# Filling the second adjacency table in four batches of edges instead of eight, and starting its scatters at batch five

## The chip, the cores and the metric

The kernel runs on one core of one Trainium2 chip. The metric is the device time of one execution in microseconds (us). Three executions of the kernel before took 3864.45, 3867.06 and 3872.6 us; the median is 3867.06 us.

## The reference, cut to what matters

3125 nodes with 256 features pass through four residual blocks: a graph convolution network of two layers, a mixture of experts that routes each node to two of eight, a gated graph network of five layers (a GRU), and a small two-expert feed-forward block. Both graph blocks sum messages over the same 50000 edges:

```
ew  = clip(abs(edge_weight), 1e-06)                   # first graph block
agg = segment_sum((dis[row] * ew * dis[col])[:, None] * xw[row], col)
agg = segment_sum(m[src] * edge_weight[:, None], dst) # third block, five times
```

## The kernel before, in words

The kernel turns both sums into dense products. It builds two tables in device memory, each 3200 by 3200 float32: `plane_a` (the weights made absolute, plus the identity, for the first block) and `plane_w` (the signed weights, for the third). A table is first filled by plain transfers, `plane_a` with zeros and a diagonal, `plane_w` with zeros, and then edge weights are added to single elements by indirect transfers that accumulate. The 50000 edges lie as 128 partitions by 392 columns (`ET`). One indirect transfer (a scatter) takes one column, 128 edges. 14 columns (`G`) are a batch, so there are 28 batches (`NB`). Within a batch, edges with the same pair of nodes are summed beforehand, so that no element is added to twice in it, and a batch on a table starts only when the batch before it on that table has landed.

Who does what up to 945 us, with the names in the code:

- VectorE compares the keys of a batch with each other (L1353 to L1361), TensorE sums the weights of equal keys, ScalarE evicts the sums, and VectorE writes the slots and values (`place`, L1364 to L1372) and raises `placed`. ScalarE also starts one transfer per batch that broadcasts the keys of a later batch to all partitions (`load_keys`, L922, 896 KB each).
- SyncE's queue holds, in order: the edges, the fill of `plane_a` (25 transfers, L332), the input x, and then the fill of `plane_w`: 100 transfers of 400 KB (L336 to L339, 128 rows of 3200 bytes each). Fill number n waits until n // FB + 1 batches of `plane_a` have landed (`scat_a`), with FB = 13: thirteen fills per batch of edges, eight batches of edges, the last with nine fills. Behind them SyncE waits until all 28 batches are placed (L347), and then loads and stores the halves of the experts' weights (`load_part`, `w_split`, L345 to L361), whose stores are also held back by counts of landed batches. Then it waits for all of `plane_a`'s scatters (L371) and streams the table into the ring `gring_lo` (L379), from which the first graph block is computed.
- GpSimd issues the scatters. Its loop over the batches (L510 to L518) waits for `placed`; from batch `FIRST_W` = 9 on it issues one single scatter to `plane_w` (L506); then it waits for the landing of the previous batch on `plane_a` and issues fourteen scatters to `plane_a` (L500). At batch 9 exactly it first waits until all 100 fills of `plane_w` have landed (`filled_w`, L513). So 19 scatters to `plane_w` are issued inside the loop. After the loop 233 more follow (up to 252 = G * W1, L519), and the last 140 are issued between the steps of the experts' block (L542).

Batches are numbered from 0 here, as in the code.

Of the kernel before, what the change touches and what calls it, by code (L numbers as in the profile page):

```python
# [25 lines left out]
NB = ET // G  # L26
UP = G * (G + 1) // 2
W1 = 18
FB, FIRST_W = 13, 9
BP, P0 = 18, 4  # L30
WB = 3
FULL = 112
# [1927 lines left out]
```

## Time and profile before

| | us |
|---|---|
| median of three runs | 3867.06 |
| the profiled execution's own time | 3872.27 |
| its span in the profile | 3870.7 |
| TensorE busy (matmul) | 3051.9 (79%) |
| VectorE busy | 2375.8 (61%) |
| ScalarE busy | 1530.7 (40%) |
| GpSimd busy | 1414.4 (37%) |

The span is the time from the first to the last instruction of the profiled execution; its own time is 1.6 us longer. Busy shares are averages over stages: during the first 945 us the tables are built, from 945 to some 1460 us the first graph block runs, to some 1940 us the experts, to 3650 us the GRU, and then the last block. A share over the whole span therefore says little of what limits a stage.

### The profile page before, as it was taken

The numbers are of one execution on the slowest core, as the hardware profiler recorded it, in microseconds if no ns is written. First come the engines' busy times: TensorE is split into PE (matmuls) and PEld (weight loads), VectorE is DVE, ScalarE is ACT, GpSimd is POOL, SyncE is SP. The second block draws the span as 40 slices with busy tenths as digits, with TensorE's granted clock in tenths as the row PEclk, the third lists the DMA queues.
The fourth block names the chain that finished last, engine by engine and source line by source line (L and its number), as shares of the span: only waits on it lengthen the run. The fifth ranks groups of instructions, "written<-read, shape, count | busy, mean of one in ns | idle before, by whom it ended". The sixth has DMA issues, their size and how long they took to land.

```text
span 3870.7 us, 54544 instructions
## 1 busy us (share of the span) xinstructions
PE 3051.9 (79%) x18100; PEld 2747.6 (71%) x18101; DVE 2375.8 (61%) x5044; ACT 1530.7 (40%) x3100; POOL 1414.4 (37%) x921
## 2 busy tenths in 40 slices
PE   2455454201999994999949999999999999999798
PEld 2444453101888883888849988998998899899677
DVE  7999996511787876555575555455545555555447
ACT  2344342110444552333334444444444444444255
POOL 1577888788877774878800000000000000000000
PEclk9999998655999996999979999999999999999889
DMA  9877335684667655535263333343433343344000
GB/s 395 265 226 196 38 48 118 188 255 79 177 166 204 181 129 172 136 86 136 33 225 125 129 119 128 119 131 117 134 127 119 127 129 122 126 132 131 37 31 29
DMA packets 378074, 538.46 MB, mean 139 GB/s; under 512 B 125779, under 2 KB 283642, under 8 KB 374458
## 3 DMA queue, kind: packets, MB, share of 16 engines
q1 hardware_dynamic: 251076, 487.82, 37.1%
q0 software_dynamic: 119088, 19.33, 8.8%
q10 hardware_dynamic: 7750, 29.17, 2.1%
q8 instruction: 100, 1.64, 0.2%
q14 instruction: 60, 0.49, 0.0%
HBM read 398.99 MB, written 137.25 MB: 139 GB/s over the span
## 4 chain that ended last, share of the span: by engine, by line
PE 44%; DVE 4%; DMA 1%; ACT 1%; issue 0%; SPq 0%; POOL 0%; ACTq 0%; DVEq 0%
PE bank L607 43%; DVE ring_lo L1702 1%; PE bank L786 1%; PE bank L855 1%; DMA yg_end<-chosen 0%; DVE gates_sb L1728 0%; ACT ring_hi L1107 0%; DVE gates_sb L1727 0%; DVE res_b L1814 0%; DVE xT L1729 0%; DVE v_lo L1759 0%; DVE stats L1780 0%; DVE stats L1817 0%; DVE nat L1789 0%; DMA past_res<-chosen 0%
## 5 line engine op out<-in xcount | busy, mean ns | idle before, releaser
L506 POOL DMA_INDIRECT plane_w<-pair,slot x392 | 658.0, 1679 | 188.4 <-issue 128.4
L500 POOL DMA_INDIRECT plane_a<-pair,slot x392 | 624.1, 1592 | 267.6 <-issue 123.4
L607 PE MATMUL bank<-ring_hi,h_hi 128*128 128x448 f32 x1750 | 652.7, 373 | 60.9 <-DVE ring_lo L1702 55.5
L1702 DVE TENSOR_TENSOR ring_lo<-ring_lo,ring_hi 128x448 fp32r<-128x448 f32 x875 | 522.8, 621 | 220.4 <-ACT ring_hi L1107 219.9
L1107 ACT ACTIVATE ring_hi<-ring_lo 128x448 fp32r<-128x448 f32 x875 | 497.3, 576 | 384.6 <-PE bank L607 378.0
L607 PE MATMUL bank<-ring_lo,h_hi 128*128 128x448 f32 x1750 | 643.5, 368 | 0.0
L607 PE MATMUL bank<-ring_hi,h_lo 128*128 128x448 f32 x1750 | 643.1, 367 | 0.0
L554 POOL DMA_DIRECT2D v_lo<-gru_v x5 | 3.6, 722 | 1388.1 <-PE bank L607 1311.9
L607 PE MATMUL bank<-gring_hi,hs_hi 128*128 128x512 f32 (+2 forms) x700 | 261.6, 374 | 256.6 <-DVE gring_lo L1417 256.6
L607 PEld LDWEIGHTS bank<-ring_hi,h_hi 128*128 128x128 f32 x1750 | 331.1, 189 | 89.8 <-DVE h_lo L1769 49.3
L1720 DVE SCALAR_TENSOR_TENSOR gates_sb<-bank,bhh,gates_sb 128x448 f32<-128x448 f32 x70 | 47.9, 685 | 516.7 <-ACT gates_sb L1131 516.7
L607 PEld LDWEIGHTS bank<-ring_hi,h_lo 128*128 128x128 f32 x1750 | 331.1, 189 | 27.6
L607 PEld LDWEIGHTS bank<-ring_lo,h_hi 128*128 128x128 f32 x1750 | 331.6, 189 | 25.9
L983 ACT ACTIVATE gring_hi<-gring_lo 128x512 fp32r<-128x512 f32 (+2 forms) x350 | 199.8, 584 | 340.4 <-DMA gring_lo<-plane_a 169.9
L607 PEld LDWEIGHTS bank<-gring_hi,hs_hi 128*128 128x128 f32 x700 | 132.5, 189 | 278.2 <-issue 256.8
L1417 DVE TENSOR_TENSOR gring_lo<-gring_lo,gring_hi 128x512 fp32r<-128x512 f32 (+2 forms) x350 | 207.6, 630 | 182.9 <-ACT gring_hi L983 174.0
L579 PE MATMUL bank<-parts,eq 128*128 x392 | 58.6, 169 | 324.5 <-DVE hit_hi L1361 302.1
L579 PEld LDWEIGHTS bank<-parts,eq 128*128 128x128 bf16 x392 | 39.3, 105 | 328.8 <-issue 328.8
L930 ACT ACTIVATE off_lo<-row,dlo_neg 128x128 f32<-128x128 f32 x392 | 151.7, 387 | 297.9 <-DVE hit_hi L1361 257.5
L607 PE MATMUL bank<-gring_lo,hs_hi 128*128 128x512 f32 (+2 forms) x700 | 257.4, 368 | 0.0
L607 PE MATMUL bank<-gring_hi,hs_lo 128*128 128x512 f32 (+2 forms) x700 | 257.3, 368 | 0.0
L1130 ACT ACTIVATE gates_sb<-bank,brz 128x448 f32<-128x448 f32 x70 | 44.4, 634 | 474.0 <-PE bank L607 474.0
(349 smaller groups left out, 6742.2 us busy)
## 6 DMA issues: line engine op xcount, KB each, us to landing
ring_lo<-plane_w SPq DMA_DIRECT2D x175, 1120.0 KB, 5.5
gring_lo<-plane_a SPq DMA_DIRECT2D x50, 1280.0 KB
plane_a<-nat SPq DMA_DIRECT2D x25, 1600.0 KB, 43.4
plane_w<-nat SPq DMA_DIRECT2D x100, 400.0 KB
w_hl<-w_split SPq DMA_DIRECT2D x16, 2048.0 KB
part_in<-in_L_ffn_W SPq DMA_DIRECT2D x16, 1024.0 KB
w_split<-part_hi SPq DMA_DIRECT2D x16, 1024.0 KB
w_split<-part_lo SPq DMA_DIRECT2D x16, 1024.0 KB
```

The lines of the kernel that those rows point to most:

```text
L500: g_.indirect_dma_start(out=plane, out_offset=bass.IndirectOffsetOnAxis(slot[:, t:t + 1], 0), in_=pair[:, k, t:t + 1], in_offset=None, com ...
L506: g_.indirect_dma_start(out=plane_w, out_offset=bass.IndirectOffsetOnAxis(slot[:, n:n + 1], 0), in_=pair[:, 0, n:n + 1], in_offset=None, c ...
L579: mm(ps_sum[c][:, g, :], eq_row(c, g, g, g + 1), parts(g, 8), start=True, stop=(g == G - 1))
L607: last = mm(ps, lhs[x], rhs[y], start=start and n == 0, stop=stop and n == 2)
L786: last = tr(turned_tile(i, t)[:, k * 128:(k + 1) * 128], xT[:, k, t * 128:(t + 1) * 128], ident[:, :])
L930: A(off_lo[:, g % 2, :], row[:, :], ACT.Square, bias=dlo_neg[:, bass.ds(n * G + g, 1)]).then_inc(lo_apart, 1)
L983: A(gring_hi[:, n % RH, 0:w_], gring_lo[:, n % RS, 0:w_].bitcast(FP32), ACT.Copy).then_inc(ring_h, 1)
L1107: A(ring_hi[:, t % HS, :], ring_lo[:, t, :].bitcast(FP32), ACT.Copy).then_inc(hi_rdy, 1)
L1130: A(gr[:, j, :], gate_ps[0][:, 0:GW], ACT.Sigmoid, bias=brz[:, j:j + 1])
L1417: V.tensor_tensor(gring_lo[:, n % RS, 0:w_], gring_lo[:, n % RS, 0:w_].bitcast(FP32), gring_hi[:, n % RH, 0:w_].bitcast(FP32), ALU.subtrac ...
L1702: V.tensor_tensor(ring_lo[:, t, :], ring_lo[:, t, :].bitcast(FP32), ring_hi[:, t % HS, :].bitcast(FP32), ALU.subtract).then_inc(lo_rdy, 1)
L1720: link(V.scalar_tensor_tensor(gr[:, j, :], gate_ps[3][:, 0:GW], bhh[:, 2 * KD + j:2 * KD + j + 1], gr[:, j, :], ALU.add, ALU.mult))
```

## The change

Two constants on one line:

```
-FB, FIRST_W = 13, 9
+FB, FIRST_W = 25, 5
```

With FB = 25, fill n of `plane_w` waits for n // 25 + 1 landed batches: 25 fills each after batches 0, 1, 2 and 3 have landed. With FIRST_W = 5 GpSimd waits for `filled_w` ahead of batch 5 and issues one scatter to `plane_w` ahead of each of the batches 5 to 27, 23 in all; 229 follow behind the loop. The number of fills, of scatters and of bytes is unchanged, and so is everything from the 253rd scatter to `plane_w` on.

## Rows read from the trace of the kernel before

**Rows 1.** Waits from 870 to 960 us: who waited for whom, total, times, longest.

```profile
PE bank L607 <- DVE gring_lo L1417: 251.2, 1, 251.2
ACT gring_hi L983 <- DMA gring_lo<-plane_a: 98.9, 2, 98.2
SPq L379 <- DMA plane_a<-pair,slot: 65.1, 1, 65.1
```

**Rows 2.** Timeline, last `plane_a` scatter and the first ring load (start, duration, engine).

```profile
941.33 1.55 POOL L500 DMA_INDIRECT plane_a<-pair,slot  x1 [0.30 <-issue]
...
944.34 24.53 SPq L379 DMA_DIRECT2D gring_lo<-plane_a  x5
```

**Rows 3.** Timeline of GpSimd: batch starts and pauses; in brackets the idle time before.

```profile
154.30 1.55 POOL L500 DMA_INDIRECT plane_a<-pair,slot  x1 [4.19 <-DMA plane_a<-pair,slot]
...
182.04 1.55 POOL L500 DMA_INDIRECT plane_a<-pair,slot  x1 [2.11 <-DMA plane_a<-pair,slot]
...
238.19 1.55 POOL L500 DMA_INDIRECT plane_a<-pair,slot  x1 [2.65 <-DMA plane_a<-pair,slot]
...
249.25 1.56 POOL L500 DMA_INDIRECT plane_a<-pair,slot  x1 [3.96 <-issue]
...
269.67 1.55 POOL L500 DMA_INDIRECT plane_a<-pair,slot  x1 [2.17 <-DMA plane_a<-pair,slot]
...
353.37 1.56 POOL L500 DMA_INDIRECT plane_a<-pair,slot  x1 [2.29 <-DMA plane_a<-pair,slot]
358.09 1.55 POOL L500 DMA_INDIRECT plane_a<-pair,slot  x1 [3.15 <-issue]
...
372.70 1.56 POOL L500 DMA_INDIRECT plane_a<-pair,slot  x1 [1.96 <-issue]
...
383.84 1.55 POOL L506 DMA_INDIRECT plane_w<-pair,slot  x1 [0.30 <-issue]
385.70 1.55 POOL L500 DMA_INDIRECT plane_a<-pair,slot  x1 [0.30 <-issue]
...
413.48 1.55 POOL L500 DMA_INDIRECT plane_a<-pair,slot  x1 [0.30 <-issue]
```

**Rows 4.** DMA issues of the page: target, source, count, KB each.

```profile
plane_w<-nat SPq DMA_DIRECT2D x100, 400.0 KB
...
front<-key_rows ACTq DMA_DIRECT2D x14, 896.0 KB
```

**Rows 5.** Windows over fill bursts: length, busy per engine, clock, DMA share, GB/s.

```profile
153.60:170.20 16.60, 5.87 (x29) 5.75 (x28) 16.45 (x44) 4.87 (x17) 13.46 (x9) 1.00 1.00 321
181.30:201.80 20.50, 10.54 (x133) 9.95 (x133) 19.68 (x60) 8.54 (x29) 16.71 (x11) 1.00 1.00 305
...
237.50:253.70 16.20, 5.65 (x27) 5.53 (x26) 16.20 (x43) 4.78 (x16) 10.03 (x7) 1.00 0.98 329
...
sum 144.50, PE 68.73 PEld 65.15 DVE 141.10 ACT 57.72 POOL 111.94; mean PE 8.59 PEld 8.14 DVE 17.64 ACT 7.21 POOL 13.99
```

**Rows 6.** The same view inside two bursts, without their beginnings.

```profile
155.20:170.20 15.00, 4.26 (x21) 4.15 (x21) 14.85 (x39) 3.37 (x12) 12.56 (x9) 1.00 1.05 336
...
300.00:315.00 15.00, 6.57 (x43) 6.37 (x40) 15.00 (x35) 5.36 (x18) 12.56 (x9) 1.00 1.08 356
```

**Rows 7.** Timeline of ScalarE's queue, key loads (six from first to last).

```profile
170.01 0.34 ACTq L922 DMA_DIRECT2D xT<-key_rows  x1
...
274.67 0.34 ACTq L922 DMA_DIRECT2D front<-key_rows  x1
```

**Rows 8.** The page's slices of 96.8 us, GB/s moved.

```profile
GB/s 395 265 226 196 38 48 118 188 255 79 177 166 204 181 129 172 136 86 136 33 225 125 129 119 128 119 131 117 134 127 119 127 129 122 126 132 131 37 31 29
```

**Rows 9.** Timeline of GpSimd, two `plane_w` scatters around the stage of the experts' weights.

```profile
633.98 1.55 POOL L506 DMA_INDIRECT plane_w<-pair,slot  x1 [0.31 <-issue]
...
859.83 1.55 POOL L506 DMA_INDIRECT plane_w<-pair,slot  x1 [0.30 <-issue]
```

**Rows 10.** Timeline of GpSimd, the last scatter behind the loop and the first gather.

```profile
1480.16 1.55 POOL L506 DMA_INDIRECT plane_w<-pair,slot  x1 [0.30 <-issue]
1505.31 1.03 POOL L525 DMA_INDIRECT xT<-tokens,idx_x  x1 [23.61 <-DVEq L1631]
```

**Rows 11.** Waits from 0 to 1000 us, VectorE for key loads.

```profile
DVE eq L1359 <- DMA front<-key_rows: 15.8, 1, 15.8
```

## The prediction

> **What bounds the kernel now.** I read the waits around the start of the first graph block first, since all of the edited code lies ahead of it. TensorE stands still for 251.2 us until its first ring tile is ready, ScalarE has waited 98.2 us for the first ring load, and SyncE's queue has stood 65.1 us on one thing only, the landing of `plane_a`'s scatters [rows 1]. The reader is to see that nothing else is late there: whatever moves the last `plane_a` scatter (941.33) moves the first ring load, three microseconds behind it [rows 2], and with it all that follows, one for one, while the move is under some 65 us. So the whole question is when GpSimd issues its 392 scatters to `plane_a`.
>
> Then the timeline of GpSimd, batch by batch. A scatter occupies it for 1.55 us and the next follows 0.3 us later, so fourteen take 25.9 us, and the next batch waits some 2 us more for the landing: batch 1 begins at 154.30 and batch 2 at 182.04, 27.74 us later. Batches 5, 6 and 7 together take from 269.67 to 353.37, 27.9 us each. From batch 9 on a `plane_w` scatter stands in front, yet from 385.70 to 413.48 it is 27.78 us: fifteen issues of 1.85 us, and the landing wait has gone. Thus one `plane_w` scatter per batch is free, because it fills a wait [rows 3]. In batches 4 and 8 there are three pauses (3.96, 3.15 and 1.96 us) that no releaser explains; all lie in or just behind a burst of fills.
>
> Last the windows over the fills. The eight bursts take 144.5 us together from their gates to their last data; a burst of thirteen takes 16.2 or 16.6 us where no key load falls into it, 20.5 us where one does [rows 5]. Today a burst ends before its batch of edges does, and the DMA engines are idle of it until the next gate; and GpSimd reaches its wait for the fills (ahead of 383.84) with all 100 long landed, so that it pauses 0.3 us [rows 3].
>
> **The change part by part.**
>
> 1. *The fills become one stream.* The first gate stays at 153.6. The next ones open when batches 1, 2 and 3 have landed, every 28 us, but 25 fills need more: thirteen took 14.6 to 15.0 us of flow (bursts of rows 5 less a lead-in of 1.6, from 153.6 to where the flow of [rows 6] begins), that is 1.14 us a fill or 28.5 us for 25, and with one key load about 33. So each gate opens before the DMA engines are through with the previous 25, and there is no gap. Length of the stream, in two ways. By times: 1.6 + 100 x 1.14 + six key loads [rows 7] x 4.1 (20.5 - 16.4) = 140.2 us. From the measured total: 144.5, less seven lead-ins of 1.6, plus one key load more than the five that fall into today's bursts, = 137.4 us. I take 139; it ends at 292.6. Bounds: with 1.12 us a fill and 3 us a key load, 132 us; with nothing saved by chaining and the sixth key load, 148.6 us. As a check by bytes: 100 x 400 KB and 6 x 896 KB [rows 4] are 46.5 MB, which is 334 GB/s, between the 305 and 329 of whole bursts and the 336 and 356 inside them [rows 5, 6].
>
> 2. *GpSimd's wait for the fills comes while they run.* Batch 4 is issued from about 240 to 270 (today 238.19 to 267.5, with its pause). There GpSimd now stands until the stream has landed, 292.6 and 1 us for the semaphore (bounds 0 and 2.7, the longest ordinary landing wait of [rows 3]). Behind it in its queue are all later scatters to both tables. One `plane_w` scatter (1.85 us) goes first, and batch 5 begins at 295.4 instead of 269.67: **+25.8 us**. What the long stream does to batches 1 to 4 costs nothing extra: even if their landing waits grow, they have until 292.6, that is 34.6 us a batch against 28. For the same reason the pause of 3.96 us in batch 4 does not count.
>
> 3. *Four more `plane_w` scatters in the loop*, ahead of batches 5 to 8. They fill the landing wait: three periods of 27.78 instead of 27.90, **-0.3 us**. Without that cover each would cost 1.85 us.
>
> 4. *No fills beside batches 5 to 8.* Batch 8 now lasts 32.33 us (353.37 to 385.70) and would last 27.78: **-4.5 us** if the two pauses come from the fills, 0 if not. I take -4.5, since between batches 9 and 17, without fills, none is seen.
>
> 5. *Four fewer scatters behind the loop*, 7.4 us of GpSimd: worth nothing. The last of them is issued at 1480.16 and GpSimd then idles 23.61 us until VectorE has the indices [rows 10]. Bounds 0 and -7.4.
>
> 6. *The others.* VectorE is ahead of the scatters and was held by a key load once only, at the start, 15.8 us [rows 11]; with two key buffers a load that takes a few us longer in the stream is hidden behind a batch of comparisons of 21 us (0; a bound of +3). SyncE has nothing behind the fills until all batches are placed, far later. The stage of the experts' weights slows the scatters: from 633.98 to 859.83 there are seven periods of 32.3 us, 31 us over the ordinary [rows 9]. Its transfers now meet the chain up to a batch earlier, but are the same in number and mostly held by counts of landed batches: 0, bounds -8 and +4.
>
> Sum: 25.8 - 0.3 - 4.5 = **+21 us**. On the profiled execution's 3872.27 us this gives 3893; it lies 5.2 us above the median of 3867.06, for which the same sum gives **3888 us**.
>
> The Trainium skill, page "DMA: Bandwidth & Descriptors", section "Specifications", puts the limit of one core's traffic with device memory at about 358 GB/s; the trace agrees so far, with 356 GB/s as the most inside a burst [rows 6]. By that figure the stream, 46.5 MB, would last an estimated 130 us, and the change would cost about 12 us.
>
> **The rivals.**
>
> - *The stream is hidden.* Not slower than before. Small bursts may understate what a long run of fills reaches: the fill of `plane_a`, longer rows in a run of 25 transfers, moved 395 GB/s over the whole first slice [rows 8]. At that rate 46.5 MB need 118 us and the stream ends at 273; batch 5 starts at about 276, +6, and less 4.8 the result is +1: 3868 us. It decides the matter if a fill takes under about 1.0 us in the stream. Against it: 3200-byte rows never passed 356 GB/s here, in any of eight bursts. The same page, section "Bandwidth", gives 425 GB/s for a 16 MB transfer and says that batching brings transfers nearer the peak; by that figure the stream would be an estimated 109 us and wholly covered. No run here shows that rate.
> - *The delay is partly made good in the weights' stage.* If the loads that VectorE's progress starts (at 643 us, unmoved) collide with fewer batches, up to 8 of the 31 us vanish: +13, 3880 us. Against it: the last stores wait for counted batches and move along.
> - *Scatters and fills hinder each other.* While the weights move, a batch takes 32.3 us on average, though they are far fewer bytes than the fills. If the stream stretches to 148.6 us and the pauses of batch 8 stay, it is 302.2 + 1 + 1.85 - 269.67 - 0.3 = +35: 3902 us. For it: bursts with a key load move only 305 GB/s. Against: the bursts were measured with the scatters in them.
> - *GpSimd's time counts after all.* With the hidden stream and 7.4 us fewer behind the loop on the path: +1 - 7.4 = -6, and -8 with better luck in the weights' stage: 3859 us. The 23.61 us of idleness speak against it.
>
> **How the numbers follow.** Forecast (+12 to +29) 0.70; scatters hindered (+30 and more) 0.09; delay partly made good (+8 to +12) 0.05; hidden stream 0.12; GpSimd's time 0.04. A measurement of this kernel can tell 0.2%, 7.7 us, from no change. So slower 0.84, same 0.12, faster 0.04. Its own range is 3879 to 3896; for eight in ten over all cases I take 3869 to 3902, from the hidden stream's edge to the hindered one.
>
> **What would show it.** Right: the fills of `plane_w` run from 153.6 to about 293 at 330 to 340 GB/s without a gap; GpSimd idles some 20 us ahead of its first `plane_w` scatter, put down to the fills; batches 5 to 8 follow at 27.8 us without pauses; the last `plane_a` scatter is issued at about 962 and the first ring load at 965; all later stages keep their lengths. Wrong: no idle time ahead of that scatter (hidden stream), batches 1 to 4 that last beyond 34.6 us, pauses that stay in batch 8, or weights' periods other than 32 us on average.

## The result and the profile after

The changed kernel takes 3885.92 us (median of six runs, 3880.66 to 3892.61) against 3866.84 us of the kernel before in runs beside it: +19.1 us, a ratio of 1.0043 with a 95% interval of 1.0032 to 1.0053. It is slower by 0.4%, clear of the noise, and the forecast of 3888 us and its range of 3869 to 3902 us hold. The profiled execution spans 3891.0 us against 3870.7, +20.3.

The waits from 870 to 990 us of the changed kernel (who waited for whom, total, times, longest) show the same picture as [rows 1]: the first block stands and waits for the ring, and for nothing else.

```profile
PE bank L607 <- DVE gring_lo L1417: 248.5, 1, 248.5
...
ACT gring_hi L983 <- DMA gring_lo<-plane_a: 100.3, 3, 98.2
```

The last `plane_a` scatter comes at 958.84 and the first ring load at 961.82, 17.5 us later than in [rows 2]. Now GpSimd's timeline of the changed kernel, the lines that answer to [rows 3] (start, duration, in brackets the idle time before and what ended it):

```profile
153.19 1.55 POOL L500 DMA_INDIRECT plane_a<-pair,slot  x1 [3.47 <-DMA plane_a<-pair,slot]
...
185.57 1.55 POOL L500 DMA_INDIRECT plane_a<-pair,slot  x1 [6.76 <-DMA plane_a<-pair,slot]
...
220.95 1.55 POOL L500 DMA_INDIRECT plane_a<-pair,slot  x1 [9.75 <-DMA plane_a<-pair,slot]
...
253.64 1.55 POOL L500 DMA_INDIRECT plane_a<-pair,slot  x1 [7.06 <-DMA plane_a<-pair,slot]
...
267.41 1.56 POOL L500 DMA_INDIRECT plane_a<-pair,slot  x1 [6.67 <-issue]
...
290.19 1.55 POOL L506 DMA_INDIRECT plane_w<-pair,slot  x1 [4.54 <-DMA plane_w<-nat]
292.04 1.55 POOL L500 DMA_INDIRECT plane_a<-pair,slot  x1 [0.30 <-issue]
...
376.64 1.55 POOL L500 DMA_INDIRECT plane_a<-pair,slot  x1 [0.30 <-issue]
...
404.58 1.55 POOL L500 DMA_INDIRECT plane_a<-pair,slot  x1 [0.44 <-DMA plane_a<-pair,slot]
```

The reader is to see two things. Batch 5 begins at 292.04, 22.4 us later than before, close to the forecast 295.4. But GpSimd stood only 4.54 us for the fills, where the prediction expected some 20. The time had gone already: the landing waits ahead of batches 2, 3 and 4 are 6.76, 9.75 and 7.06 us where they were 2.11, 2.25 and 2.65 (+16.6 us), and the pause in batch 4 is 6.67 us, not 3.96 (+2.7). Then batch 8 lasts 27.94 us (376.64 to 404.58) instead of 32.33: its two pauses are gone.

The windows over the stream of fills (length, busy per engine, clock, DMA share, GB/s) of the changed kernel show a nearly steady flow; SyncE issues the 100 fills from 152.5 to 279.4, and the data end at about 288:

```profile
155.00:185.00 30.00, 14.15 (x150) 13.44 (x150) 29.59 (x78) 11.63 (x39) 20.11 (x13) 1.00 1.09 343
185.00:215.00 30.00, 14.21 (x219) 13.25 (x220) 28.75 (x94) 11.88 (x40) 21.66 (x14) 1.00 1.08 354
215.00:245.00 30.00, 17.41 (x186) 16.56 (x183) 29.18 (x79) 14.51 (x49) 20.12 (x13) 1.00 1.02 335
...
285.00:290.00 5.00, 0.00 (x0) 0.00 (x0) 5.00 (x10) 0.09 (x1) 0.65 (x1) 1.00 0.68 187
290.00:295.00 5.00, 0.00 (x0) 0.00 (x0) 4.97 (x19) 0.00 (x0) 4.20 (x3) 1.00 0.16 0
```

Windows of 30 us hide something that shorter ones show. The flow falls where one group of 25 fills ends and the next begins: slightly at 185, and to a quarter at 220 and at 253:

```profile
219.50:221.00 1.50, 1.50 (x9) 1.50 (x8) 1.50 (x4) 1.17 (x4) 0.05 (x1) 1.00 0.25 99
...
252.50:254.00 1.50, 0.84 (x7) 0.66 (x7) 1.08 (x8) 0.39 (x1) 0.36 (x1) 1.00 0.26 102
```

SyncE issued the 25th fill at 178.0 and the 26th only at 184.86; the third and fourth groups begin at 220.23 and 252.92. So each group waited at its gate until the batch of edges beside the group before had landed, and that batch landed just when that group's data were through (185.57, 220.95 and 253.64 above are the moments at which GpSimd goes on). In this stretch a batch of edges lasts as long as its 25 fills.

Behind the ring load everything keeps its length to within 2 us (last load of the `plane_w` ring 3590.6, before 3574.3: +16.3) until the end of the GRU. There, in these two executions, two groups of 36 products take 10.33 and 8.94 us, where the kernel before took 7.58 and 7.69; the chains of waits of the changed kernel show

```profile
3638.23 10.33 PE bank L607 x36
...
3651.32 8.94 PE bank L607 x36
```

and the window over them (its last three numbers are the granted clock, the DMA share and GB/s)

```profile
3638.00:3661.00 23.00, 20.00 (x80) 17.74 (x80) 1.48 (x3) 1.82 (x4) 0.00 (x0) 0.79 0.28 120
```

The granted clock is 0.79 on average there, so that part of the window ran at the lower of the two levels (1.2 and 2.4 GHz), and 1.00 over the same groups of the kernel before. That is 4.0 us of the span's 20.3, seen in one execution each. Whether it belongs to the change is not shown: of the runs below, the profiles of e1 (10.40 and 9.15 us) and e3 (9.14 and 8.97) show it in both groups, those of e5 and e6 in the first, those of e2, e4, e7 and e8 in neither, and what sets it no run tells.

### The profile page after: what moved, and what is told of

Read it like the earlier page. It is cut to its first block, busy times and chain, and to the rows that moved or that the text cites. A ratio compares the mean times of both kernels' runs of the same rounds, so it can differ in the third digit from the quotient of the medians.

```text
span 3891.0 us, 54540 instructions
## 1 busy us (share of the span) xinstructions
PE 3059.7 (79%) x18100; PEld 2753.8 (71%) x18101; DVE 2375.3 (61%) x5044; ACT 1530.5 (39%) x3100; POOL 1420.1 (36%) x921
## 4 chain that ended last, share of the span: by engine, by line
PE 44%; DVE 4%; DMA 1%; ACT 1%; issue 0%; SPq 0%; POOL 0%; ACTq 0%; DVEq 0%
PE bank L607 43%; DVE ring_lo L1702 1%; PE bank L786 1%; PE bank L855 1%; DMA yg_end<-chosen 0%; DVE gates_sb L1728 0%; ACT ring_hi L1107 0%; DVE gates_sb L1727 0%; DVE res_b L1814 0%; DVE xT L1729 0%; DVE v_lo L1759 0%; DVE stats L1780 0%; DVE stats L1817 0%; DVE nat L1789 0%; DMA fb<-in_L_ffn_b1T 0%
```

## The experiments

Eight kernels, each timed against the kernel before on the same chip. Each changes only the lines shown and computes everything.

| kernel | edit (FB, FIRST_W) | last `plane_a` scatter | median us | before | ratio (95%) |
|---|---|---|---|---|---|
| before | 13, 9 | 941.33 | | | |
| changed | 25, 5 | 958.84 | 3885.92 | 3866.84 | 1.0043 (1.0032 to 1.0053) |
| e1 | 25, 9 | 959.11 | 3888.58 | 3868.70 | 1.0046 (1.0033 to 1.0059) |
| e2 | 13, 8 | 954.65 | 3883.67 | 3868.70 | 1.0040 (1.0027 to 1.0053) |
| e3 | 7, 5, FW = 1 | 976.56 | 3903.27 | 3868.70 | 1.0082 (1.0069 to 1.0095) |
| e4 | 13, 17, gates 8 later | 945.49 | 3880.83 | 3868.70 | 1.0026 (1.0015 to 1.0036) |
| e5 | 20, 6 | 944.68 | 3872.36 | 3869.92 | 1.0008 (0.9999 to 1.0016) |
| e6 | 17, 7 | 936.54 | 3869.52 | 3869.92 | 0.9999 (0.9991 to 1.0008) |
| e7 | 15, 8 | 937.37 | 3867.42 | 3869.92 | 0.9995 (0.9987 to 1.0004) |
| e8 | 13, 8, gates 1 earlier | 937.99 | 3867.09 | 3869.92 | 0.9994 (0.9985 to 1.0002) |

The third column is from each profile, one execution each; it leaves out the variation that later stages add. The expectations give times against a kernel before of 3867 us. Beside the runs it took 3868.70 (e1 to e4) and 3869.92 (e5 to e8), so differences are compared, not times.

### e1: the stream without the early wait

```
-FB, FIRST_W = 13, 9
+FB, FIRST_W = 25, 9
```

> FB = 25, FIRST_W = 9: the fills as in the changed kernel, but GpSimd's wait for them stays ahead of batch 9. Theory W (the prediction's): the price is GpSimd's wait for the fills, and batches 1 to 4 are slowed only because there is slack; then batch 5 begins within 5 us of the kernel before (270 to 275) and the time is 3864 to 3870 us. Theory L, formed on the changed kernel's trace, where batches 1 to 4 took 32.4, 35.4, 32.7 and some 36 us and GpSimd waited only 4.5 us for the fills: the price is the landing waits (6.8, 9.8 and 7.1 us instead of 2.1 to 2.7) and the pause of 6.7 us beside the stream; then batch 5 begins at 287 to 291 and the time is 3880 to 3885 us.

Measured: +19.9 us, the cost of the whole change; theory L had said +13 to +18. GpSimd's timeline:

```profile
186.00 1.55 POOL L500 DMA_INDIRECT plane_a<-pair,slot  x1 [6.70 <-DMA plane_a<-pair,slot]
...
221.53 1.57 POOL L500 DMA_INDIRECT plane_a<-pair,slot  x1 [9.90 <-DMA plane_a<-pair,slot]
...
253.94 1.55 POOL L500 DMA_INDIRECT plane_a<-pair,slot  x1 [6.71 <-DMA plane_a<-pair,slot]
...
267.76 1.56 POOL L500 DMA_INDIRECT plane_a<-pair,slot  x1 [6.72 <-issue]
...
289.61 1.55 POOL L500 DMA_INDIRECT plane_a<-pair,slot  x1 [3.59 <-DMA plane_a<-pair,slot]
...
376.47 1.55 POOL L500 DMA_INDIRECT plane_a<-pair,slot  x1 [1.87 <-issue]
...
391.10 1.56 POOL L500 DMA_INDIRECT plane_a<-pair,slot  x1 [1.96 <-issue]
```

There is no wait for the fills here, yet batches 1 to 3 last as long as in the changed kernel, batch 4 takes 35.67 us where the kernel before took 31.48, and batch 5 begins only 2.4 us earlier than in the changed kernel. Theory W falls: taking the wait away gives back 2.4 us at batch 5, of which nothing is left at batch 9, since here the two pauses of batch 8 are back (1.87 and 1.96 us) although no fill runs then. Theory L holds: the long stream makes the scatters land late, and that alone costs what the change costs. The gates show the same lock-step as in the changed kernel: the second to fourth groups of fills start at 185.28, 220.81 and 253.22.

### e2: the wait alone

```
-FB, FIRST_W = 13, 9
+FB, FIRST_W = 13, 8
```

> FB = 13, FIRST_W = 8: the fills in eight bursts as before, GpSimd's wait for them one batch earlier, while the last nine fills run. Theory W: GpSimd idles from 351 until these have landed at about 369, some 16 us, less the 4.5 us of pauses in batch 8 that now fall into the wait: +11 to +14 us, 3878 to 3881 us. Theory L says the same of this wait, since here it is no longer than the fills; if a wait of GpSimd there did not reach the end of the kernel, the time would be 3862 to 3870 us.

Measured: +15.0 us, a little more than the 11 to 14 expected. GpSimd's first `plane_w` scatter:

```profile
368.75 1.55 POOL L506 DMA_INDIRECT plane_w<-pair,slot  x1 [16.34 <-DMA plane_w<-nat]
```

The bursts and the landing waits are nearly as before (2.1 to 3.5 us), and the wait of 16.34 us moves the last `plane_a` scatter by 13.3 us. So a wait of GpSimd there does reach the end in full; in the changed kernel it is merely short, because the late landings have used up the same time. The wait and the late landings are two ways to the same delay, and each is enough alone.

### e3: longer rows, a faster stream

```
-FB, FIRST_W = 13, 9
+FB, FIRST_W = 7, 5
-FW = 4
+FW = 1
```

> FW = 1, FB = 7, FIRST_W = 5: plane_w is filled by 25 transfers of 1600 KB with rows of 12800 bytes, seven per batch of edges in four batches. Theory R (rate): such rows moved 395 GB/s in the fill of plane_a, so the stream of 46.5 MB ends at about 273 instead of 290, landing waits shrink with it, batch 5 begins near 276 to 280: 3868 to 3873 us. Theory S (sharing): the scatters' elements wait behind one packet of a fill each time, and a packet of 12800 bytes holds an engine longer than one of 3200; the landing waits beside the stream are 10 us and more, and the time is 3885 us or more.

Measured: +34.6 us, the slowest of all. The windows of the stream and GpSimd's timeline:

```profile
155.00:185.00 30.00, 15.77 (x158) 15.01 (x157) 29.56 (x78) 13.16 (x44) 21.65 (x14) 1.00 1.04 400
...
265.00:275.00 10.00, 0.10 (x1) 0.00 (x0) 10.00 (x26) 0.26 (x1) 6.16 (x4) 1.00 1.03 410
...
285.00:290.00 5.00, 0.84 (x4) 0.71 (x4) 5.00 (x10) 0.27 (x1) 3.59 (x3) 1.00 0.13 0
```

```profile
190.14 1.55 POOL L500 DMA_INDIRECT plane_a<-pair,slot  x1 [9.52 <-DMA plane_a<-pair,slot]
...
227.72 1.55 POOL L500 DMA_INDIRECT plane_a<-pair,slot  x1 [11.80 <-DMA plane_a<-pair,slot]
...
264.97 1.55 POOL L500 DMA_INDIRECT plane_a<-pair,slot  x1 [11.62 <-DMA plane_a<-pair,slot]
...
285.80 1.56 POOL L500 DMA_INDIRECT plane_a<-pair,slot  x1 [13.72 <-issue]
...
304.35 1.55 POOL L506 DMA_INDIRECT plane_w<-pair,slot  x1 [0.31 <-issue]
```

The flow reaches 400 GB/s over the first 30 us and 410 where only fills run, but it ends at about 285 in place of 288, the landing waits rise to 9.5 to 11.8 us and the pause to 13.7 us. GpSimd comes to its wait for the fills at 304, long after they have landed, and pauses 0.31 us. Theory R's rate was right in the bursts and its conclusion wrong: this is no stream that could end at 273. Seven of these transfers hold the bytes of 28 of the shorter ones, and between two groups the engines stand idle until the batch has landed:

```profile
187.00:190.00 3.00, 0.00 (x0) 0.00 (x0) 3.00 (x11) 0.00 (x0) 0.00 (x0) 1.00 0.16 0
224.50:227.50 3.00, 0.00 (x0) 0.00 (x0) 3.00 (x5) 0.00 (x0) 0.00 (x0) 1.00 0.19 0
```

Again each batch lands behind its burst, here some 3 us behind (batches 2 and 3 begin at 190.14 and 227.72). Theory S's forecast holds, 10 us and more apart from the 9.52 of batch 2. The burst beside a batch also grew from 25 to 28 fills' worth of bytes, so the time alone would not settle the cause; the packets do (queue, packets, MB, share of the engines; q1 is SyncE's queue, q0 is GpSimd's; first from 161 to 185 us, then from 185 to 188):

```profile
q1 hardware_dynamic: 753, 8.61, 91.1%
q0 software_dynamic: 749, 0.00, 4.9%
...
q0 software_dynamic: 1267, 0.01, 65.3%
q1 hardware_dynamic: 47, 0.40, 32.8%
```

While fills run, one packet of the scatters goes with each packet of the fills, 31 per us of either. A scatter is 144 packets (a batch of fourteen 2016) and GpSimd issues one in 1.85 us, 78 packets per us. So they pile up, and 1267 of batch 1's 2016 move only in the last 3 us, when the burst's data end. In the changed kernel, with the shorter rows, the scatters' packets move at 88 per us from 196 to 212 (1406 beside 2055 of the fills), little above the 78 at which they are issued, but hardly at all around a key load: 144 from 191 to 195.5, nearly all of them in the first of these microseconds, beside 188 of the fills. Batch 2 has two key loads beside it and the longest landing wait, 9.75 us.

### e4: the same bursts, eight batches later

```
-FB, FIRST_W = 13, 9
+FB, FIRST_W = 13, 17
...
-                sp.wait_ge(scat_a, 16 * G * (n // FB + 1))
+                sp.wait_ge(scat_a, 16 * G * (n // FB + 9))
```

> FB = 13 with gates n // 13 + 9 and FIRST_W = 17: the eight bursts run beside batches 9 to 16 instead of 1 to 8, and all plane_w scatters start eight batches later, so that eight more stand behind the loop (14.8 us, under the 23.6 us that GpSimd idles there). Theory P (the pauses of GpSimd belong to places in its instruction stream and show where a fill runs then): the pauses at the 61st, 114th and 122nd scatter go, others of 2 to 4 us come beside batches 9 to 16, and the time stays within 5 us of before. Rival: the pauses belong to the bursts' order in time, the 4th and the 8th burst, and then come again in batches 12 and 16 with 4 and 5 us. Either way 3862 to 3872 us; if no pause comes, 3858 us.

GpSimd's timeline, all its pauses up to batch 17 that end by no releaser, and one landing wait:

```profile
247.60 1.56 POOL L500 DMA_INDIRECT plane_a<-pair,slot  x1 [1.77 <-issue]
...
355.03 1.55 POOL L500 DMA_INDIRECT plane_a<-pair,slot  x1 [1.92 <-issue]
...
369.59 1.56 POOL L500 DMA_INDIRECT plane_a<-pair,slot  x1 [1.90 <-issue]
...
469.39 1.55 POOL L500 DMA_INDIRECT plane_a<-pair,slot  x1 [4.80 <-DMA plane_a<-pair,slot]
...
493.44 1.56 POOL L500 DMA_INDIRECT plane_a<-pair,slot  x1 [2.07 <-issue]
...
589.95 1.55 POOL L500 DMA_INDIRECT plane_a<-pair,slot  x1 [3.86 <-issue]
```

The pauses are at the 61st, 114th and 121st scatter, as in the kernel before, and at the 181st and 227th. The first, third and fourth are sixty scatters apart, the second and fifth 113. So they belong to places in GpSimd's instruction stream (theory P), but they do not need a fill: without one they last 1.8 to 2.1 us, beside a burst 3.2 to 4.0, in the long streams 6.7 and 13.7. The expectation that the first three vanish without fills was wrong. The rival's batches 12 and 16 did each show a pause, of 2.07 and 3.86 us against the 4 and 5 expected, but the rival does not explain the three that stayed. In every kernel, from the first `plane_w` scatter on no such pause of over 0.6 us is seen up to the stage of the weights; why, no run tells.

The time was a miss: +12.1 us where I had said within 5. The last `plane_a` scatter is only 4.2 us late. But eight more scatters stand behind the loop, the last at 1523.93, and the first gather follows it at once:

```profile
1523.93 1.55 POOL L506 DMA_INDIRECT plane_w<-pair,slot  x1 [5.42 <-issue]
1525.78 1.02 POOL L525 DMA_INDIRECT xT<-tokens,idx_x  x1 [0.30 <-issue]
```

Against [rows 10] the idle 23.61 us are gone. The expectation priced eight scatters at 1.85 us each, 14.8 us in all. Behind the loop they are further apart, 2.3 us on average in the kernel before (233 in 538.8 us), and here the 241 took 578.4 us, 39.6 more, with several waits of 5 to 6 us near the end. GpSimd's tail is on the path: the first load of the `plane_w` ring comes 14.6 us later than before, 10.4 more than the last `plane_a` scatter. That slack is thinner than its number. The twelve executions spread from 3870.91 to 3887.82 us and the profiled one is the slowest, so the tail need not cost this much each time.

### e5, e6, e7: twenty, seventeen and fifteen fills per batch

```
-FB, FIRST_W = 13, 9
+FB, FIRST_W = 20, 6
```

> FB = 20, FIRST_W = 6: five bursts of twenty fills. A burst lasts 1.6 + 20 x 1.14 + 4 (a key load) = 28.4 us, just over a batch of 27.8. Theory Q (quiet end): the landing wait of a batch grows only where the fills reach past its last scatter, here in all of batches 1 to 5, by 1 to 5 us each, +5 to +15 in sum, the pause in batch 4 grows to 5 to 7 (+2), and the two pauses of batch 8 go since plane_w scatters come earlier (-4.4): 3872 to 3880 us. Theory V (volume): the loss goes with the fills beyond thirteen beside each batch; seven of the twelve of the changed kernel and its 22 us without the pauses: +13 - 4.4, 3877 us. The two differ in the runs with 17 and 15.

```
+FB, FIRST_W = 17, 7
```

> FB = 17, FIRST_W = 7: six bursts of seventeen, 25 us with a key load, so that the fills end 2 to 3 us before the batch. Theory Q: landing waits of 2 to 4 us, sum +0 to +4; pauses of batch 8 gone, -4.4: 3864 to 3868 us. Theory V: 4/12 of 22, +7 - 4.4: 3871 us.

```
+FB, FIRST_W = 15, 8
```

> FB = 15, FIRST_W = 8: seven bursts of fifteen, 22.7 us with a key load, and plane_w scatters from batch 8 on with no wait for the fills. Theory Q: landing waits as in the kernel before, pauses of batch 8 gone: -4.4, 3864 us. Theory V: 2/12 of 22, +4 - 4.4: 3868 us. If the pauses of batch 8 stay although a plane_w scatter comes ahead of it, 3868 us by Q too.

GpSimd's timeline in e5, batch starts 2 and 4 and the first `plane_w` scatter:

```profile
183.15 1.60 POOL L500 DMA_INDIRECT plane_a<-pair,slot  x1 [3.79 <-DMA plane_a<-pair,slot]
...
243.79 1.55 POOL L500 DMA_INDIRECT plane_a<-pair,slot  x1 [6.40 <-DMA plane_a<-pair,slot]
...
304.99 1.55 POOL L506 DMA_INDIRECT plane_w<-pair,slot  x1 [3.94 <-DMA plane_w<-nat]
```

And in e6, batches 2, 3 and 7, with one window between two bursts:

```profile
181.63 1.55 POOL L500 DMA_INDIRECT plane_a<-pair,slot  x1 [2.27 <-DMA plane_a<-pair,slot]
...
209.48 1.55 POOL L500 DMA_INDIRECT plane_a<-pair,slot  x1 [2.23 <-DMA plane_a<-pair,slot]
...
324.88 1.55 POOL L500 DMA_INDIRECT plane_a<-pair,slot  x1 [0.30 <-issue]
```

```profile
178.50:181.50 3.00, 1.27 (x6) 1.15 (x6) 3.00 (x7) 0.26 (x1) 0.86 (x1) 1.00 0.15 0
```

Seventeen fills leave only 3 quiet us before the batch has landed, and that is enough: all landing waits of batches 2 to 6 are 2.1 to 2.6 us in e6 and 2.1 to 2.8 in e7. With twenty the waits are 3.79, 2.83 and 6.40 us for batches 2, 3 and 4, and back to 2.26 for batch 5, and with twenty-five 6.76, 9.75 and 7.06. The loss does not go with the number of fills but begins where the burst reaches the end of the batch: theory Q, against V, which wanted +7 for seventeen before the pauses. Q had put the loss in e5 too high: the pause in batch 4 is 3.97 us, not 5 to 7, the last `plane_a` scatter is 3.4 us late, and the time is +2.4 us (no difference by its interval), just under the +5 to +13 expected. With the two pauses of batch 8 gone, the last `plane_a` scatter of e6 comes 4.8 us earlier than before and that of e7 4.0. In the whole time e6 (-0.4 us) and e7 (-2.5) show no difference, which is near Q's forecast (-3 to +1, and -3) and under V's (+4 and +1) by less than these runs can tell (intervals 0.9991 to 1.0008 and 0.9987 to 1.0004), so the gain of 4 to 5 us is seen in the timeline of one execution each and not in the measured time.

### e8: every burst one batch earlier

```
-FB, FIRST_W = 13, 9
+FB, FIRST_W = 13, 8
...
-                sp.wait_ge(scat_a, 16 * G * (n // FB + 1))
+                sp.wait_ge(scat_a, 16 * G * (n // FB))
```

> FB = 13, gates n // 13, FIRST_W = 8: eight bursts as before, but each one batch earlier, the first beside batch 0, right behind the load of x. No batch has more fills beside it than before. If the early start of the plane_w scatters is what removes the two pauses of batch 8, the last plane_a scatter is issued 4 to 5 us earlier and the time is 3862 to 3866 us. If the pauses stay, 3867 to 3870 us.

The last `plane_a` scatter comes at 937.99, 3.3 us earlier than before; batch 8 lasts 27.8 us without a pause. That is the first branch of the expectation, with 3.3 us in place of its 4 to 5. The median of 3867.09 against 3869.92 lies within the interval of no change (0.9985 to 1.0002). Its ratio is the lowest of all tried, by too little to be called faster; the experiments point to no version that beats the kernel before by a measurable amount.

## Why the prediction was right, and where it was not

- **The bound.** Right: the last `plane_a` scatter moved by 17.5 us, the first ring load by 17.5, the last `plane_w` ring load by 16.3.
- **Step 1, one stream.** Right in length: 100 fills, ended at about 288 against 292.6 forecast (bounds 286 to 302). Wrong in the reason for the missing gaps: the gates do not open before the engines are through with the previous 25 fills. Each opens just as they are, because the batch of edges beside them lands no sooner; the gaps are only short. The limit of about 358 GB/s that the prediction takes from the Trainium skill ("DMA: Bandwidth & Descriptors", section "Specifications") did not show: e3 moved 400 GB/s over 30 us. The 395 GB/s of [rows 8] already spoke against the prediction's words that the trace agrees. The measurement decides.
- **Step 2, GpSimd's wait is the price.** The sum was near (batch 5 at 292.04, forecast 295.4), the mechanism only half right. What holds: the wait does end batch 4 in the changed kernel. The data end at about 288.5 and the waiting scatter starts at 290.19, within the bounds for the semaphore. And the wait alone would have cost the same, an estimate: it would have held batch 5 until then even with every batch at its old length; e2 shows such a wait reaching the end. What failed is the sentence that what the long stream does to batches 1 to 4 costs nothing extra. It is hidden behind the wait only while the wait stands. It took 16.6 us of landing waits and 2.7 us of pause, and left the wait for the fills 4.5 us, 2.4 more than the landing wait that it replaced. e1 has the stream without the wait and loses the same; e3 reaches the wait long after the fills landed and loses more. That both ways give one number is no accident: a batch lands when its 25 fills are through, so batch 4's landing (289 in e1) and the stream's end (288) are set by the same four groups of fills. The prediction had the length of a group right (about 33 us with a key load; batches 1 to 3 last 32.4, 35.4 and 32.7), but did not see that it was also the length of a batch. The rival "scatters and fills hinder each other" had the missing mechanism, but was priced as an addition to the wait instead of beside it.
- **Step 3, a free `plane_w` scatter.** Right: batches 5 to 7 last 28.93, 27.85 and 27.82 us, 0.9 more in sum than before instead of 0.3 less.
- **Step 4, -4.5 us for batch 8.** The size was right (32.33 to 27.94), the cause wrong: not the missing fills but the `plane_w` scatters ahead of the batch go with it. e1 has no fills there and keeps 3.8 us of pauses.
- **Step 5, the tail is worth nothing.** Right here: GpSimd idles 27.4 us before the first gather. e4 shows that the reverse doesn't hold.
- **Step 6, the rest.** The seven periods of the weights' stage take 221.6 us (655.72 to 877.35) instead of 225.9, -4.2, inside the bounds of -8 and +4; the batch ahead of them took 29.4 instead of 27.8, +1.6.

Sum as it came: +22.4 at batch 5, +0.9 in batches 5 to 7, -4.4 in batch 8, +1.3 in batches 9 to 16 from small landing waits, -2.7 from batch 17 on: +17.5 at the last `plane_a` scatter.

## What to carry to other kernels

If small dependent transfers run beside a bulk transfer, pace the bulk so that each portion ends a few microseconds before the small ones must have landed: here seventeen 400 KB fills per 28 us were free and twenty-five cost 20 us. When two things end at about the same time, a sum by either comes out right; ask of each what would remain if the other were taken away, and run that, and ask whether one of them holds the other. Look at a steady flow in short windows: those of 30 us hid the gates. A slack read from one profile is good for its own mix of traffic only.

## What the runs showed of the hardware

- GpSimd stands 2.1 to 2.8 us for the landing of a batch of scatters of 128 elements when the fills have ended by then (e6, e7), 6.7 to 9.9 us beside groups of 25 fills with 3200-byte rows at 335 to 354 GB/s, and 9.5 to 11.8 us beside groups of seven with 12800-byte rows at up to 410 GB/s. In the long bursts the batch lands about when the burst's data end (changed, e1), some 2 us behind it (e5) or some 3 us behind it (e3).
- Beside 12800-byte rows the scatters' packets went one for one with those of the fills, 749 beside 753 in 24 us, while GpSimd issued 78 per us; the remaining 1267 of the batch moved within 3 us at the burst's end (e3).
- GpSimd pauses at fixed places of its stream of scatters (the 61st in every kernel, the 121st and 181st where no `plane_w` scatter had come yet), 1.8 to 2.1 us with no bulk transfer beside it, 3.2 to 4.0 beside a burst, 6.7 and 13.7 in the long bursts. What it fetches or waits for there no run tells.
